# Softmax of one attention: ScalarE takes exponentials and row sums from PSUM head by head, values weighed in float16 parts

## The reference

```python
xn = _ln(x, lnx_g, lnx_b)
yn = _ln(y, lny_g, lny_b)                      # here y is x
q = jnp.einsum('bsc,hcd->bhsd', xn, wq)
k = jnp.einsum('btc,hcd->bhtd', yn, wk)
v = jnp.einsum('btc,hcd->bhtd', yn, wv)
a = jax.nn.softmax(jnp.einsum('bhsd,bhtd->bhst', q, k) * D ** (-0.5), axis=-1)
if causal:
    mask = (jnp.arange(t)[None, :] > jnp.arange(s)[:, None]).astype(a.dtype)
    a = a * mask
o = jnp.einsum('bhst,bhtd->bhsd', a, v)
o = o.transpose(0, 2, 1, 3).reshape(x.shape[0], x.shape[1], H * D)
x_out = x + o @ li1_w + li1_b
```

## Time and profile before

| | us |
|---|---|
| median of 3 runs | 5575.47 |
| lowest, highest | 5569.66, 5575.83 |
| the profiled execution | 5589.97 |
| its span | 5588.1 |

### The profile page before, as it was taken

How to read it: one execution, slowest core, us unless ns; L and a number is a source line. 1 busy time by engine, 2 the same in 40 slices (tenths; PEclk the granted TensorE clock), 3 DMA queues, 4 the chain that set the end, 5 groups by cost and what they waited for, 6 DMA issues and landing times. The chain is left out here.

```text
span 5588.1 us, 132733 instructions
## 1 busy us (share of the span) xinstructions
PE 4842.0 (87%) x41659; PEld 3572.6 (64%) x41659; DVE 3953.4 (71%) x9897; ACT 2700.3 (48%) x5454; POOL 2176.0 (39%) x3095
## 2 busy tenths in 40 slices
PE   7888998999952799688889989889898899998898
PEld 4555667888852466455566667767776677776554
DVE  5666876777766333677767768989886789897544
ACT  4545774555530233454555545555553455554344
POOL 5443001100027100776533357777776433333200
PEclk9989999999975899899999999999998999999878
DMA  1002400000011333100100000000000000000000
GB/s 40 8 7 66 209 0 6 5 5 5 5 56 44 114 135 133 35 23 22 30 2 0 0 6 0 0 0 0 0 0 7 3 2 2 2 2 7 0 14 17
DMA packets 109012, 141.38 MB, mean 25 GB/s; under 512 B 35832, under 2 KB 83256, under 8 KB 103996
## 3 DMA queue, kind: packets, MB, share of 16 engines
q1 hardware_dynamic: 100544, 120.88, 6.3%
q0 software_dynamic: 8192, 16.79, 1.0%
HBM read 47.44 MB, written 58.72 MB: 19 GB/s over the span
## 5 line engine op out<-in xcount | busy, mean ns | idle before, releaser
L2213 POOL TENSOR_TENSOR l3a_probs<-l3a_probs,l3a_later 128x512 f32<-128x512 f32 x256 | 320.6, 1280 | 4.9 <-DVE l3a_total L2401 4.9
L2199 POOL TENSOR_TENSOR l3a_keys<-l3a_kT,head 128x2048 f32<-128x2048 f32 x64 | 230.4, 3600 | 232.2 <-ACT l3a_kT L2326 232.2
L181 POOL TENSOR_TENSOR l1x_ve<-l1x_mv,eps 128x1 f32<-128x1 f32 x64 | 12.2, 190 | 646.7 <-DVE l1x_mv L173 646.7
L2261 PE MATMUL l3a_scores<-l3a_keys,l3a_qT 128*128 128x512 f32 x512 | 255.5, 601 | 4.2 <-POOL l3a_keys L2199 4.2
L1696 POOL TENSOR_TENSOR l2f_hid<-l2f_prod,l2f_route 128x512 f32<-128x512 f32 x128 | 152.1, 1193 | 254.7 <-DVE l2f_prod L1843 251.3
L309 PE MATMUL l3a_po<-l3a_vals,l3a_probsT 128*128 128x32 f32 x2048 | 251.0, 271 | 0.1
L309 PEld LDWEIGHTS l3a_po<-l3a_vals,l3a_probsT 128*128 128x128 f32 x2048 | 250.2, 194 | 0.4 <-ACT l3a_probsT L290 0.4
L265 ACT ACTIVATE l3a_probs<-l3a_probs 128x512 f32<-128x512 f32 x256 | 161.7, 632 | 180.7 <-DVE l3a_probs L256 175.7
L1582 PE MATMUL l1e_h<-l1e_xhi,l1f_parts 128*128 128x512 f16 x640 | 205.1, 382 | 9.7 <-DVE l1e_gated L1640 8.2
L2199 POOL TENSOR_TENSOR l3c_keys<-l3c_kT,head 128x1232 f32<-128x1232 f32 x64 | 144.0, 2250 | 156.7 <-ACT l3c_kT L2326 156.7
L295 DVE SCALAR_TENSOR_TENSOR l1x_loT<-l1x_turned,l1x_hiT 77x512 f16<-77x512 f32 x256 | 168.9, 679 | 48.9 <-ACT l1x_hiT L288 48.9
(11 more groups left out here) (581 smaller groups left out, 17155.9 us busy)
## 6 DMA issues: line engine op xcount, KB each, us to landing
l_rows<-l0f_zeros SPq DMA_DIRECT2D x34, 1024.0 KB, 27.1
l1f_parts<-l1f_split SPq DMA_DIRECT2D x40, 512.0 KB, 3.6
l1e_x_in<-l_rows SPq DMA_DIRECT2D x40, 256.0 KB, 2.8
l1f_down<-l1f_w SPq DMA_DIRECT2D x40, 256.0 KB, 2.4
l_rows<-l1e_y_out SPq DMA_DIRECT2D x40, 256.0 KB, 2.7
l1f_w<-in_L_W SPq DMA_DIRECT2D x16, 256.0 KB, 3.6
out_x<-x_res SPq DMA_DIRECT2D x16, 256.0 KB, 2.0
x_res<-in_x SPq DMA_DIRECT2D x1, 3840.0 KB, 12.3
```

Source lines behind the costliest of these rows:

```text
L2199: pool.tensor_tensor(keys[it.par][:, :, :, :], kT[it.par][:, :, :].unsqueeze(2).to_broadcast([P, J, G4, T]), g.head32[:, :].unsqueeze(1).u ...
L2213: pool.tensor_tensor(v, v, later[:, :].unsqueeze(1).to_broadcast([P, 4, T]), ALU.mult).then_inc(s_masked, 1)
L2261: pe.matmul(scores[c][:, 0:G4 * T], qT[it.par][:, c, :], keys[it.par][:, c, :, :].rearrange("p h t -> p (h t)"), start=True, stop=True).th ...
```

## The change

In l3a only, `Softmax` now runs with `direct` and `split`.

- The queries are fetched with a factor of minus the scale, so the scores come out negated and scaled; VectorE takes the minimum of each head in place of the maximum.
- There is no shift. ScalarE reads the scores from PSUM, a head (128x128) at a time, computes exp(minimum - score) with the minimum as a pointer bias, and puts out the row sum by `accum_out`. So sixteen instructions stand for four, and the four row sums of VectorE are gone.
- A score bank is free once the exponentials have read it (`s_exp`), not after the shift.
- `fetch_p` writes a float16 high part, VectorE computes the rest (`remainder`), and the values are split the same way (`values` on VectorE); `weigh` does three float16 products per head, 48 per element in place of 16 float32 ones.
- `turn_p` of group c waits for the remainder of two groups earlier, and `turn` for the rest of the values (`s_vlo`) of the element before.
- VectorE's order is new; `remainder` has lag 5 and `values` lag 3. POOL's mask waits for the exponentials instead of the sums.

```diff
     def exponential(self, act, it, c):
         ...
+    def exponential_of_bank(self, act, it, c, total):
+
+        a, b = self.first[c], self.first[c + 1]
+        act.wait_ge(self.s_max, nth(it, self.nb, c))
+        if (due := nth(it, self.nc_, ago=2)) is not None:
+            act.wait_ge(self.s_turn, due)
+        for h in range(a, b):
+            last = act.activation(self.probs[it.par][:, h, :], self.view(c)[:, h - a, :], ACT.Exp,
+                                  bias=self.mx[it.par][:, h:h + 1], scale=-1.0, accum_out=total[it.par][:, h:h + 1])
+        last.then_inc(self.s_exp, 1)
...
-        sm = Softmax(st, g, scores, [4] * 4, T, scale, turned, split=not first)
+        sm = Softmax(st, g, scores, [4] * 4, T, scale, turned, split=True, direct=first)
...
-                    pool.wait_ge(s_sum, nth(it, 4, c))
+                    pool.wait_ge(sm.s_exp, nth(it, 4, c))
...
-                        pe.wait_ge(s_vals if first else s_vlo, due)
+                        pe.wait_ge(s_vlo, due)
...
-                        pe.wait_ge(sm.s_shift, due)
+                        pe.wait_ge(sm.s_exp if first else sm.s_shift, due)
...
+                    if first:
+                        act.activation(dst, pa[:, :], ACT.Copy, scale=-scale).then_inc(s_qT, 1)
...
                 def divide(it):
                     p = it.par
-                    dve.wait_ge(s_sum, nth(it, 4))
+                    if first:
+                        dve.wait_ge(sm.s_exp, nth(it, 4))
...
                 if first:
                     steps.update(stats1=(stats1, 0), stats2=(stats2, 1), stats3=(stats3, 2))
-                    names = ("hat stats3 maximum0 stats2 shift0 maximum1 add shift1 maximum2 maximum3 shift2 shift3 sum0 "
-                             "sum1 stats1 sum2 sum3 divide")
+                    names = ("hat stats3 remainder0 maximum0 stats2 maximum1 remainder1 add maximum2 remainder2 maximum3 stats1 "
+                             "remainder3 divide values")
```

More of the change, by code:

```diff
@@ L213, with __init__ @@
 class Softmax:
-    def __init__(self, st, g, banks, heads_of_bank, keys, scale, ps_turn, split=False):
+    def __init__(self, st, g, banks, heads_of_bank, keys, scale, ps_turn, split=False, direct=False):
+        self.direct = direct
         self.g, self.banks, self.keys, self.scale = g, banks, keys, scale
@@ L246, in maximum @@
         if (due := nth(it, self.nb, ago=2)) is not None:
-            dve.wait_ge(self.s_shift, due)
-        dve.tensor_reduce(self.mx[it.par][:, a:b], self.view(c), AX, ALU.max).then_inc(self.s_max, 1)
+            dve.wait_ge(self.s_exp if self.direct else self.s_shift, due)
+        dve.tensor_reduce(self.mx[it.par][:, a:b], self.view(c), AX, ALU.min if self.direct else ALU.max).then_inc(self.s_max, 1)
     def shift(self, dve, it, c):
@@ L2146, in l3_attention @@
         xT, yT = st.sb2("xT", [P, P]), st.sb2("yT", [C, T])
-        qT, kT, vals = st.sb2("qT", [P, J, P]), st.sb2("kT", [P, J, T]), st.sb2("vals", [T, HEADS * D])
+        qT, kT = st.sb2("qT", [P, J, P]), st.sb2("kT", [P, J, T])
         keys = st.sb2("keys", [P, J, G4, T])
-        if not first:
-            vhi, vlo = st.sb2("vhi", [T, HEADS * D], F16), st.sb2("vlo", [T, HEADS * D], F16)
-            s_vhi, s_vlo = st.sem("s_vhi"), st.sem("s_vlo")
+        vhi, vlo = st.sb2("vhi", [T, HEADS * D], F16), st.sb2("vlo", [T, HEADS * D], F16)
+        s_vhi, s_vlo = st.sem("s_vhi"), st.sem("s_vlo")
         total, recip = st.sb2("total", [P, HEADS]), st.sb2("recip", [P, HEADS])
@@ L2268, in weigh @@
                     if c == 0:
-                        pe.wait_ge(s_vals if first else s_vlo, nth(it))
+                        pe.wait_ge(s_vlo, nth(it))
                         if (due := nth(it, ago=1)) is not None:
@@ L2273, in values_of @@
                         cols = slice(h * D, (h + 1) * D)
-                        return vals[it.par][:, cols] if first else (vhi[it.par][:, cols], vlo[it.par][:, cols])
+                        return vhi[it.par][:, cols], vlo[it.par][:, cols]
                     sm.times_values(pe, it, c, lambda h: po[:, h * D:(h + 1) * D], values_of)
@@ L2319, in fetch_q @@
                         act.wait_ge(sm.s_scores, due)
-                    act.copy(qT[it.par][:, :, :].rearrange("p j t -> p (j t)"), pa[:, :]).then_inc(s_qT, 1)
+                    dst = qT[it.par][:, :, :].rearrange("p j t -> p (j t)")
+                    if first:
+                        act.activation(dst, pa[:, :], ACT.Copy, scale=-scale).then_inc(s_qT, 1)
+                    else:
+                        act.copy(dst, pa[:, :]).then_inc(s_qT, 1)
                 def fetch_k(it):
@@ L2331, in fetch_v, with exponential @@
                         act.wait_ge(sm.s_values, due)
+                    act.activation(vhi[it.par][:, :], pa[0:T, :], ACT.Copy, scale=SPLIT).then_inc(s_vhi, 1)
+                def exponential(it, c):
                     if first:
-                        act.copy(vals[it.par][:, :], pa[0:T, :]).then_inc(s_vals, 1)
+                        if c == 0 and (due := nth(it, ago=2)) is not None:
+                            act.wait_ge(s_recip, due)
+                        sm.exponential_of_bank(act, it, c, total)
                     else:
-                        act.activation(vhi[it.par][:, :], pa[0:T, :], ACT.Copy, scale=SPLIT).then_inc(s_vhi, 1)
+                        sm.exponential(act, it, c)
                 def fetch_o(it):
@@ L2342, in fetch_o @@
                     act.activation(oT[it.par][:, :, :].rearrange("p j t -> p (j t)"), po[:, :], ACT.Copy,
-                                   scale=1.0 if first else 1.0 / (SPLIT * SPLIT_EXP)).then_inc(s_oT, 1)
+                                   scale=1.0 / (SPLIT * SPLIT_EXP)).then_inc(s_oT, 1)
                 steps = {**numbered("fetch_p", lambda it, c: sm.fetch(act, it, c), 4, 5),
-                         **numbered("exp", lambda it, c: sm.exponential(act, it, c), 4, 4), "fetch_x": (fetch_x, 3),
+                         **numbered("exp", exponential, 4, 4), "fetch_x": (fetch_x, 3),
                          "fetch_q": (fetch_q, 3), "fetch_k": (fetch_k, 3), "fetch_v": (fetch_v, 3), "fetch_o": (fetch_o, 6)}
@@ L2423, in add @@
                     dve.tensor_tensor(y, po[:, 0:P], y, ALU.add).then_inc(s_out, 1)
-                steps = {**numbered("maximum", lambda it, c: sm.maximum(dve, it, c), 4, 4),
-                         **numbered("shift", lambda it, c: sm.shift(dve, it, c), 4, 4), **numbered("sum", row_sum, 4, 4),
+                steps = {**numbered("maximum", lambda it, c: sm.maximum(dve, it, c), 4, 4), "values": (value_remainder, 3),
+                         **numbered("remainder", lambda it, c: sm.remainder(dve, it, c), 4, 5),
                          "hat": (hat, 3 if first else 2), "divide": (divide, 5 if first else 6), "add": (add, 6)}
@@ L2429, in _ @@
                     steps.update(stats1=(stats1, 0), stats2=(stats2, 1), stats3=(stats3, 2))
-                    names = ("hat stats3 maximum0 stats2 shift0 maximum1 add shift1 maximum2 maximum3 shift2 shift3 sum0 "
-                             "sum1 stats1 sum2 sum3 divide")
-                else:
-                    steps.update(stats_z=(stats_z, 2), values=(value_remainder, 3),
-                                 **numbered("remainder", lambda it, c: sm.remainder(dve, it, c), 4, 5))
+                    names = ("hat stats3 remainder0 maximum0 stats2 maximum1 remainder1 add maximum2 remainder2 maximum3 stats1 "
+                             "remainder3 divide values")
+                else:
+                    steps.update(stats_z=(stats_z, 2), **numbered("sum", row_sum, 4, 4),
+                                 **numbered("shift", lambda it, c: sm.shift(dve, it, c), 4, 4))
                     names = ("divide maximum0 remainder0 shift0 stats_z add remainder1 maximum1 shift1 maximum2 remainder2 "
```

2 lines of the change are left out of this document (added).

## The result

The changed kernel takes 6170.9 us (median of 4 runs, 6168.4 to 6173.4) where the kernel before takes 5575.7 (4 runs, 5569.7 to 5579.4) on the same chip: a ratio of 1.1063, 95% interval 1.1048 to 1.1077. It is 595 us slower; 6185 was predicted. The profiled execution took 6173.4, with a span of 6170.4, against 5590.0 and 5588.1 before.

A forecast was written before the change was run, and what follows sets the result against it. VectorE bound the old kernel at 14.4 us a pass; a ring of waits would set the new one: 14.9 us plus 6.8 of exponentials plus 2.4 of low clock, 24.1. Over 63 periods +611 us, 6185 us; range 5950 to 6340.

The forecast's parts named there:

- E: ScalarE's time for one bank of four heads' exponentials with row sums: 1.7 us (1.2 to 2.5), 0.42 a head.
- add: VectorE's step between remainder1 and maximum2, two instructions of 0.29 us less an overlap: 0.53 us.
- the clock: TensorE standing still twice a pass runs weigh3, values and score0 at the low clock: +2.4 us a pass.
- The ring: Closed loop of waits, VectorE and ScalarE taking turns, one pass long: 21.7 us, 24.1 with low clock; 6185 us, chance 0.50.
- VectorE's own work: VectorE sets the old pace of 14.4 us; its own work falls by 1.8 us a pass, to 12.6.
- TensorE's gain decides nothing: Weighing in float16 products frees TensorE by about 2 us per element, without deciding the pace.
- POOL costs nothing: POOL's drops wait for the exponentials instead of the sums; its 11 us of work has room in a 20 us pass.
- Before, only divide stood between them: In the old kernel only divide, once a pass, stood between VectorE and ScalarE; now they take turns.
- The VectorE bound: Rival: VectorE stays the bound at 12.6 us a pass, 113 us less, 5462 us; chance 0.07.
- ScalarE's sum: Rival: ScalarE's own work bounds the pass, no ring: 12.4 to 15.6 us, 5460 to 5650 us; chance 0.03.
- The ring at full clock: Rival: the loop of waits with TensorE at full clock throughout: 21.7 us a pass, 6035 us; chance 0.24.
- Dear write-outs: Rival: ring with a bank's exponentials near 2.5 us, or TensorE low throughout: 27 us, 6370 us; chance 0.16.

The follow-up runs named there:

- the queues opened: All four queues of the changed kernel put in the second attention's order: 5701.0 us; the same order with float32 weighing and no remainders: 5737.9 us.
- a single swap: POOL's spread of the keys moved ahead of the second causal product, against the kernel with all four queues reordered (5701.0 us): 5651.1 us.
- the first reordered kernel: Changed kernel with only VectorE's queue reordered, each maximum ahead of the remainder that waits for a fetch: 5966.4 us, ratio 1.070.

## Why the prediction was right, and where it wasn't

The mechanism is as predicted, and the time within 14 us. That it is so close is luck: three terms of the sum were off and nearly cancel (E -1.25 us, add +2.5, the clock -1.1). Nor does the rest of the sum hold as it stands: the 63 periods grew by 573 us and not by 611, and the drain, which had no term, added 15.0. The ring's pieces, from start to start in the timeline above (the parts between 3721.99 and the next exp2 from the same view's later rows), against the prediction's steps with its handovers:

| piece | predicted | measured |
|---|---|---|
| turn to remainder0 | 3.3 | 3.28 |
| remainder0, maximum0 | 1.3 | 1.33 |
| four banks of exponentials, 4E | 6.8 | 5.55 |
| fetch_q, fetch_k, fetch_p1 | 1.6 | 1.67 |
| remainder1, add, maximum2 | 1.8 | 4.34 |
| fetch_p2 to the end of remainder3 | 3.1 | 3.28 |
| weigh3 and the values at full clock | 1.6 | 1.5 |
| fetch_v, values, hat | 1.8 | 1.94 |
| the low clock | 2.4 | 1.0, and 0.3 in the row above |
| other handovers | 0.4 | in the rows above |
| together | 24.1 | 23.9 |

- **What bounded it before, and VectorE's own work**: right as far as the rows go: it was 90% busy and hardly waited, though no run cut its work alone. Its busy time falls from 12.9 us a pass (90% of 14.4) to 12.2 (52% of 23.5), of which 2.5 is add standing; so its work falls by 3.2 us where 1.8 was predicted. The rest is time in which it stood before, too: by form, 3400 to 4100 of the kernel before, one addition lasted more than four times as long as its like, and one product more than twice:

```profile
L2376 DVE TENSOR_TENSOR l_z<-l3a_xa,l3a_ln_b 128x128 f32 x49 | 65.0, 1327 | 6.5
L2116 DVE TENSOR_SCALAR l3a_xa<-x_res,l3a_n_mv,l3a_n_rs 128x128 f32 x48 | 40.3, 840 | 0.0
...
L2420 DVE TENSOR_TENSOR l_y<-l_z,l3a_bias 128x128 f32 x48 | 13.4, 280 | 0.0
```

  In the kernel after the first two take 292 and 338 ns (the third, add's first half, is the one that is held there). That POOL can hold VectorE was thus to be seen in the trace of before; the prediction read past it.
- **TensorE's gain decides nothing**: right for the kernel as it is. With the queues opened it is worth 37 us.
- **ScalarE, E**: mis-sized. 1.7 us a bank was taken, 1.39 is measured, 0.35 us a head instead of 0.42 and near the low end (0.29). The exponential's 0.36 was right (0.37); the write-out was taken at a small copy's price and overlap, and is hidden for more than half. This is -1.25 us a pass. The 387 ns that the prediction worked out as an estimate from the Trainium skill ("ScalarE: Activation LUTs", section "What ACT_TABLE_LOAD costs") are 18 more than the 369 of the trace.
- **remainder1, add, maximum2**: the failed step. It priced add at 0.53 us by rows of before, in which nothing of POOL lay beside it. The new order puts it under the spread of the keys, and it takes 2.78 + 0.29: +2.5 us a pass, shown by the run that only moves it (-2.2, and 0.37 of new wait).
- **The clock**: half right. TensorE falls to 0.50 after its wait at weigh0, and values takes 0.95 longer. Score0 and turn_o run low as well, 1.92 and 0.75 us in the timeline, but they put off turn by 0.3 us and not by 1.2: score0 starts beside fetch_v (3715.20 against 3715.44), VectorE's values and hat end only at 3717.02, and turn follows at 3717.38. That is some 1.3 in place of 2.4. The run that keeps TensorE busy shows the 0.95 in the values' rows, and there turn starts at hat's end.
- **POOL costs nothing**: right for its queue in this kernel (it waits 9.6 us a pass), wrong in that its spread holds add. And once the first ring is open, POOL's order is worth 50 us by a single swap.
- **"Before, only divide stood between them"**: misread. ScalarE's exponentials waited for VectorE's shifts before as well (138.6 us); what is new is that VectorE waits for ScalarE's fetches in return.
- **The rivals.** The VectorE bound, on the other side, is refuted by 52% busy. ScalarE's sum falls with it (46%). The ring at full clock was predicted at 21.7; with TensorE kept busy it is 22.98, since add lengthens it. Dear write-outs: refuted by the run without row sums; TensorE low throughout: it is low in 10 of 23.9 us.

What the prediction didn't see is that the ring isn't the only one. The theory in its form would have had the first reordered kernel at 5680 to 5740, and it came at 5966; four links were found on the way down to 75 us of loss: VectorE's maxima behind remainders, add under the spread, weigh0 behind add, the spread behind two causal products. Reordering takes back 520 of 595 us (6171 to 5651). What holds the last 75 us isn't settled: in that kernel no engine is over 82% busy, and POOL still waits 3.3 us a pass for the first exponential (149.8 us in 45 passes); whether another order would pass below 5576 wasn't tried.

## What to carry to other kernels

When an edit splits one step into a chain that goes back and forth between engines, write down the queues and follow who releases whom once round before adding up work: here the work fell and a pass grew from 14.4 to 23.5 us. Price each step where the new order puts it, with its neighbours on the other engines, not where it stood. And when the order is at fault, expect several rings: take the waits of each reordered kernel anew, since the first cut shows only the next link.
